# Second attention's preparation: each product of the keys' folded weights directly followed by one of the values

## The chip, the cores and the metric

One core of a Trainium2 chip runs the whole program. The metric is the time of one execution on the device in microseconds (us); the kernel before took 4541.19 us in the median of three runs (4521.63, 4541.19 and 4542.01 us).

## The reference

Four layers follow each other on 8192 tokens of 256 numbers (4 sequences of 2048): an attention with random features, a feed-forward network whose operands are rounded to blockwise FP4, a softmax attention with rotated and low-rank keys and values, and a routed network of 8 experts. The change touches the third layer's inputs only:

```python
q = (x @ wq.T).reshape(b, s, NH, HD).transpose(0, 2, 1, 3)
k = (x @ wk_a.T @ wk_b.T).reshape(b, s, NH, HD).transpose(0, 2, 1, 3)
v = (x @ wv_a.T @ wv_b.T).reshape(b, s, NH, HD).transpose(0, 2, 1, 3)
q = _apply_decoupled_rope(q, cosf, sinf, DROPE)
k = _apply_decoupled_rope(k, cosf, sinf, DROPE)
scores = jnp.einsum('bhqd,bhkd->bhqk', q, k) / np.float32(np.sqrt(HD))
attn = jax.nn.softmax(scores, axis=-1)
```

## The kernel before, in words

`make_plan` (it calls `prep_order` and the other order generators) writes one list of steps. Every engine then goes through that list and issues the steps that have a part for it, strictly in the list's order; semaphores alone tie the engines together. So a step's place in the list is its place on each of the queues.

**Preparation of the second attention.** For each sequence b (0 to 3), in four chunks c of 512 tokens: `pt` transposes the input (two steps), `pa` makes the 64 + 64 latent rows of keys and values (`lat`, rows 0 to 63 for the keys, 64 to 127 for the values), `px` a part of the router's logits, `pp` the queries ("q") and keys ("k") of 128 of the 256 columns (ht is 0 or 1), `ps` splits the float32 result `pres` into three bfloat16 parts on POOL (L1900 to L1906) and stores them with six DMAs from SP, and `pv` makes the values of 128 tokens (j is 0 to 3) and stores them (`vst`, `vdr`). `pp` for the keys multiplies `wkR[0:64]` with `lat[0:64]`, so it stands in the array's rows 0 to 63 and streams 512 columns; `pv` multiplies `lat[64:128]` with `wvb[64:128]`, rows 64 to 127, 256 columns. Each float32 product is recorded as two LDWEIGHTS and two MATMULs. All of these are recorded at one helper's line, L764 (L767 for transposes); they are told apart by their tiles: `lat,wkR` is `pp` of the keys and `wkR,lat` is `pv` (`wvb` and `wkR` share a buffer).

**Where these steps run.** `prep_order` yields small lists; each call of `beside()` or `background()` puts the next one, here called a *slot*, into the plan. A chunk takes 14 slots. Sequence 0 is prepared beside the feed-forward network: from tile T = 20 on there are two slots for each of the 64 tiles T, slot A after the transposes `tt` and ahead of `up`, slot B after `dn`. Sequence 1 starts in the stage that finds the first row maxima (`M` on PE, `MR` on DVE at L1607), 20 slots ahead of the attention's main loop, and goes on in it; sequences 2 and 3 run in the main loop wholly. The main loop has 1024 steps in 16 groups n of 64; a step is `S S M M S S V B` on PE: four score products `S`, each with an exponential on ACT (L1356), two `M`, one `V` (eight MATMULs, four of them side by side) and the slot B, in every other step.

**Banks and waits.** Every `S`, `R1`, `pt`, `pa`, `px`, `pp` and `pv` is an *A step*: PE writes one PSUM bank and ACT empties it. In the main loop they rotate over three banks, and PE waits until ACT has emptied that of three A steps before. Beside the network there is one bank (6), and PE waits until ACT has emptied that of the A step just before:

```python
w.wait_ge(act_A, max(0, a_no[step] - (1 if beside_ffn(step) else 3)))
```

ACT's copy of a `pp` into `pres` also waits until POOL has finished the `ps` before:

```python
w.wait_ge(pool_ps, 4 * (at["ps", b, c, qk] - 1))
```

POOL's `ps` itself waits until the six DMAs of the `ps` before have landed, and `vst` has three buffers, each free when its store has landed. The rows of maxima that an `S` needs come through `R1` (PE, ACT), `R2` (POOL, then eight DMAs `QS<-mrow` from SP, L2082); a group's operands come through `fetch` (SP, L2093 and L2094). `oe` multiplies on POOL (L1844) and waits for the DMA `den<-rd`.

Of the kernel before, what the change touches and what calls it, by code (L numbers as in the profile page):

```python
# [127 lines left out]
def prep_order(b):  # L128

    for c in range(4):  # L130
        for k in range(2):
            yield [("pt", b, c, k)]
        yield ([("pl", *divmod(4 * b + c + 1, 4))] if b and 4 * b + c + 1 < 16 else []) + [("pa", b, c)]
        yield [("px", b, c)]
        for i, w in enumerate("qk"):
            for ht in range(2):
                yield [("pp", b, c, w, ht)]
            yield [("ps", b, c, w)]
            for j in range(2):
                yield [("pv", b, c, 2 * i + j)]  # L140
    yield [("prepared", b)]


# [90 lines left out]
def make_plan():  # L234
# [63 lines left out]
    def beside():  # L298
        units = next(side, None)
        if units:  # L300
            plan.extend(units)
            prepared.update(u[1] for u in units if u[0] == "prepared")
            if 0 in prepared:
                plan.extend(("fm", 0, i) for i in range(4))

    side = prep_order(0)

    for T in range(-1, NT + 7):
# [57 lines left out]


    bg.append(prep_order(1))
    while (0, 0) not in rows:
        maximum()  # L370
# [8 lines left out]
    for step in range(1025):  # L379
        n, st = divmod(step, 64)  # L380
        if st == 0 and n < 16:
            b, g = groups[n]
            if g == 0 and 0 < b < 3:
                bg.insert(0, prep_order(b + 1))
# [1883 lines left out]
```

## Time and profile before

| | |
|---|---|
| Times of three runs, us | 4521.63, 4541.19, 4542.01 |
| Profiled execution, span, us | 4519.8 |
| PE busy | 4297.7 us, 95% |
| DVE busy | 3480.9 us, 77% |
| ACT busy | 2811.6 us, 62% |
| POOL busy | 976.4 us, 22% |
| Chain that ended last | PE 68%, DVE 12%, DMA 3%, issue 2% |

Busy time of PE is the union of its records, in which a product's latency is counted; what a product costs the engine is the distance from its start to the next one's. In the timeline a row gives start, length, engine, line, operation, tiles and how many instructions were merged; in brackets the idle time of the engine ahead of it and what ended it. The idle time of PE's weight loads (PEld) costs nothing while PE multiplies.

### The profile page before, as it was taken

What the parts mean: (1) busy time and instruction counts of PE and PEld (TensorE: products, weight loads), DVE (VectorE), ACT (ScalarE), POOL (GpSimd) and SP (SyncE); (2) the same over time, 40 slices, a digit from 0 to 9 for tenths busy, and PEclk for the clock granted to TensorE, in tenths of its full rate; (3) what the DMA queues carried; (4) which work ended last, traced back from release to release, by engine and by line L of the source; (5) the groups of instructions that cost most, each with busy time, mean ns of one, the idle gap of its engine ahead of it and who ended that gap; (6) DMA issues with size and microseconds to landing.
All of it is one profiled execution on the core that took longest, in us unless ns stands there. A gap on an engine that the chain in (4) does not pass through costs nothing.

```text
span 4519.8 us, 66262 instructions
## 1 busy us (share of the span) xinstructions
PE 4297.7 (95%) x25817; PEld 1630.7 (36%) x25820; DVE 3480.9 (77%) x3858; ACT 2811.6 (62%) x5305; POOL 976.4 (22%) x957
## 2 busy tenths in 40 slices
PE   8899889999989999999999999999999999999896
PEld 5555446666622222222222222222222232222285
DVE  3555789888887788987778888777888988888332
ACT  4333333343347788887777777777777767788721
POOL 3333434454121100001221111111110001000223
PEclk9999999999989999999999999999999999999998
DMA  3102000122133212113232221423222122221232
GB/s 112 35 29 66 20 11 15 65 68 93 57 100 116 69 70 71 42 68 101 99 113 75 82 75 48 136 92 110 67 72 84 45 75 64 71 75 65 95 120 54
DMA packets 230277, 330.49 MB, mean 73 GB/s; under 512 B 36870, under 2 KB 171464, under 8 KB 227912
## 3 DMA queue, kind: packets, MB, share of 16 engines
q1 hardware_dynamic: 227084, 318.40, 21.3%
q0 software_dynamic: 2880, 7.87, 0.9%
q8 instruction: 203, 3.33, 0.3%
q14 instruction: 110, 0.90, 0.1%
HBM read 218.71 MB, written 98.04 MB: 70 GB/s over the span
## 4 chain that ended last, share of the span: by engine, by line
PE 68%; DVE 12%; DMA 3%; issue 2%; POOL 1%; ACT 1%; SPq 1%; POOLq 0%; DVEq 0%; another core or an unknown queue 0%; ACTq 0%
PE ps L764 67%; DVE mx L1607 4%; PE ps L767 2%; DMA pk<-Ob 1%; DVE hn L1428 1%; DVE stat L1434 1%; DVE hn L1586 1%; DVE hn L1581 1%; DMA x2d<-eb 1%; DVE hs L1420 0%; DMA rd<-pk 0%; DMA QS<-mrow 0%; SPq L2082 0%; ACT Pb L1356 0%; DVE eb L1445 0%
## 5 line engine op out<-in xcount | busy, mean ns | idle before, releaser
L1607 DVE TENSOR_REDUCE mx<-ps 128x1 f32<-128x1024 f32 x2048 | 2406.6, 1218 | 423.4 <-PE ps L764 420.2
L1356 ACT ACTIVATE Pb<-ps 128x512 f32<-128x512 f32 x4096 | 2202.5, 596 | 515.1 <-PE ps L764 511.6
L764 PE MATMUL ps<-QS,KS 98*128 98x512 bf16 x4096 | 1248.8, 386 | 17.5 <-ACT Pb L1356 7.7
L764 PE MATMUL ps<-Pb,VA 128*32 128x512 f32 x8192 | 1095.1, 607 | 0.1
L764 PE MATMUL ps<-KM,QM 64*128 64x512 bf16 x4096 | 654.9, 388 | 44.6 <-DVE mx L1607 42.7
L764 PEld LDWEIGHTS ps<-QS,KS 98*128 98x128 bf16 x4096 | 259.6, 98 | 1089.1 <-ACT Pb L1356 907.5
L764 PEld LDWEIGHTS ps<-KM,QM 64*128 64x128 bf16 x4096 | 179.7, 93 | 598.0 <-issue 351.9
L764 PEld LDWEIGHTS ps<-Pb,VA 128*32 128x32 f32 x8192 | 161.3, 108 | 401.4 <-issue 400.4
L1911 POOL CAST mrow<-mres 16x128 bf16<-16x128 f32 x64 | 18.4, 287 | 1238.7 <-ACT mres L1192 1238.7
L764 PE MATMUL ps<-wdT,hT 128*128 128x256 f32 (+1 forms) x768 | 193.8, 395 | 19.3 <-DVE X L1592 19.3
L1514 DVE RECIPROCAL rB<-ps 128x512 f32<-128x512 f32 x28 | 94.0, 3357 | 107.0 <-PE ps L764 106.7
L1844 POOL TENSOR_TENSOR den<-Ob,den 128x512 f32<-128x512 f32 x64 | 81.6, 1275 | 412.9 <-DMA den<-rd 412.9
L764 PEld LDWEIGHTS ps<-wdT,hT 128*128 128x128 f32 (+1 forms) x768 | 140.5, 192 | 72.7 <-issue 50.5
L764 PE MATMUL ps<-wgT,xqT 128*128 128x352 f32 x512 | 164.4, 464 | 0.0
L764 PE MATMUL ps<-wuT,xqT 128*128 128x352 f32 x512 | 161.9, 459 | 0.0
L1900 POOL CAST parts<-pres 128x1024 bf16<-128x1024 f32 x32 | 37.7, 1177 | 479.6 <-ACT pres L1192 474.0
L1837 POOL TENSOR_SCALAR vpe<-mv 128x4 f32<-128x4 f32 (+1 forms) x52 | 12.6, 242 | 592.4 <-DVE mv L1438 592.2
L1213 ACT ACTIVATE phi<-ps 128x1024 f32<-128x1024 f32 x64 | 65.5, 1024 | 114.1 <-PE ps L764 114.1
L764 PEld LDWEIGHTS ps<-wuT,xqT 128*128 128x128 f32 x512 | 97.3, 190 | 54.2
L1565 DVE TENSOR_TENSOR hh<-ps,sg 128x704 f32<-128x704 f32 x64 | 56.5, 882 | 77.5 <-PE ps L764 77.5
L1192 ACT ACTIVATE pres<-ps 128x512 f32<-128x512 f32 x64 | 38.1, 597 | 124.5 <-PE ps L764 121.2
L1502 DVE TENSOR_TENSOR qs<-qs 32x512 f32<-32x512 f32 x128 | 97.0, 758 | 21.6 <-ACT qs L1255 19.3
(235 smaller groups left out, 4312.3 us busy)
## 6 DMA issues: line engine op xcount, KB each, us to landing
QM<-qd SPq DMA_DIRECT2D x128, 256.0 KB
KM<-kd SPq DMA_DIRECT2D x128, 256.0 KB
qd<-parts SPq DMA_DIRECT2D x96, 256.0 KB, 2.7
kd<-parts SPq DMA_DIRECT2D x96, 256.0 KB, 2.7
QS<-qd SPq DMA_DIRECT2D x64, 384.0 KB
KS<-kd SPq DMA_DIRECT2D x64, 384.0 KB
vdr<-vst SPq DMA_DIRECT2D x64, 256.0 KB, 3.1
den<-rd SPq DMA_DIRECT2D x64, 256.0 KB
```

Of the source, the lines that this page charges most:

```text
L764: return eng.matmul(out, a, b, start=start, stop=stop, skip_group_check=skip)
L767: return eng.transpose(out, a, ident[0:n, 0:n])
L1213: eng.activation(phi[n % 3], bank(1, 2), ACT.Exp, bias=0.0, scale=1.0).then_inc(act_phi, 1)
L1356: eng.activation(Pb[(u - 1) % 9], o, ACT.Exp, bias=0.0, scale=0.25).then_inc(act_A, 1)
L1428: eng.tensor_tensor(blk(xn), blk(x), wide(rs, n // 16, 16), ALU.mult).then_inc(own, 1)
L1434: d = eng.bn_stats(stat[:, i % 4, j, :], x[:, j, :])
L1502: d = eng.tensor_tensor(qs[C % 2][g][64 * k + 32 - 32 * g:64 * k + 64 - 32 * g, ht, :], x, x, ALU.mult)
L1514: eng.reciprocal(f["rB"], bank(b7)).then_inc(dve_rec, 1)
L1565: eng.tensor_tensor(hh[p % 2][:, 704 * b:704 * b + 704].rearrange("p (a b) -> p a b", a=2), bank(2, 2).rearrange("p (a b) -> p a b", a=2)[ ...
L1581: eng.scalar_tensor_tensor(out=hn[i], in0=hc, scalar=LEAST, in1=hn[i], op0=ALU.max, op1=ALU.add).then_inc(dve_qh, 1)
L1607: eng.tensor_reduce(mx4[qc % 2][:, 4 * i + q, h:h + 1], o, AX, ALU.max).then_inc(dve_D, 1)
L1844: eng.tensor_tensor(den, Ob, den, ALU.mult).then_inc(pool_at, 1)
```

## The change

Only the order of `prep_order` changes. Each of the keys' two `pp` steps comes together in one slot with one of the first two `pv` steps, `pp` first. `pv` 0 and 1 stood between the queries' `ps` and the keys' first `pp`; now they stand behind the `pp` steps, which come two slots sooner after the queries' `ps`. The keys' `ps` and `pv` 2 and 3 follow as before. A chunk takes 12 slots in place of 14. No instruction is added or removed.

```diff
             yield [("px", b, c)]
-        for i, w in enumerate("qk"):
-            for ht in range(2):
-                yield [("pp", b, c, w, ht)]
-            yield [("ps", b, c, w)]
-            for j in range(2):
-                yield [("pv", b, c, 2 * i + j)]
+        for ht in range(2):
+            yield [("pp", b, c, "q", ht)]
+        yield [("ps", b, c, "q")]
+        for ht in range(2):
+            yield [("pp", b, c, "k", ht), ("pv", b, c, ht)]
+        yield [("ps", b, c, "k")]
+        for j in range(2, 4):
+            yield [("pv", b, c, j)]
     yield [("prepared", b)]
```

## Rows read from the trace of the kernel before

**Rows 1.** The chain that ended last, shares of the span by engine.

```profile
PE 68%; DVE 12%; DMA 3%; issue 2%; POOL 1%; ACT 1%; SPq 1%; POOLq 0%; DVEq 0%; another core or an unknown queue 0%; ACTq 0%
```

**Rows 2.** Busy time by stretch: us, then each engine's, PEclk, DMA share, GB/s.

```profile
core 0: us, PE busy (x) PEld busy (x) DVE busy (x) ACT busy (x) POOL busy (x), PEclk, DMA share, GB/s
800.00:1100.00 300.00, 293.42 (x1203) 194.68 (x1202) 249.54 (x263) 115.00 (x265) 154.03 (x91) 0.98 0.22 74
1265.00:1320.00 55.00, 44.87 (x179) 14.31 (x183) 46.09 (x41) 17.85 (x35) 19.88 (x15) 0.75 0.35 118
2060.00:2372.00 312.00, 311.95 (x1780) 80.57 (x1778) 239.17 (x214) 235.79 (x460) 64.07 (x56) 1.00 0.34 110
```

**Rows 3.** Timeline of the main loop, around a `pv` in slot B.

```profile
2161.15 0.70 PE L764 MATMUL ps<-wkR,lat 64*128 64x256 f32 x2
2161.78 0.61 PE L764 MATMUL ps<-QS,KS 98*128 98x512 bf16 x2
...
2166.14 1.28 POOL L1844 TENSOR_TENSOR den<-Ob,den 128x512 f32<-128x512 f32 x1 [7.42 <-DMA den<-rd]
...
2167.01 0.70 PE L764 MATMUL ps<-wkR,lat 64*128 64x256 f32 x2
```

**Rows 4.** Timeline of the main loop, around a `pp` of the keys.

```profile
2170.68 2.18 ACT L1356 ACTIVATE Pb<-ps 128x512 f32<-128x512 f32 x4 [0.45 <-PE ps L764]
...
2172.88 1.12 PE L764 MATMUL ps<-lat,wkR 64*128 64x512 f32 x2
...
2173.93 0.61 PE L764 MATMUL ps<-QS,KS 98*128 98x512 bf16 x2
2174.10 0.60 ACT L1192 ACTIVATE pres<-ps 128x512 f32<-128x512 f32 x1 [1.24 <-PE ps L764]
...
2174.47 0.61 PE L764 MATMUL ps<-KM,QM 64*128 64x512 bf16 x4
2174.59 2.06 ACT L1356 ACTIVATE Pb<-ps 128x512 f32<-128x512 f32 x4
...
2175.01 0.62 PE L764 MATMUL ps<-QS,KS 98*128 98x512 bf16 x2
```

**Rows 5.** Timeline beside the network, a `pv` in slot B and one in A.

```profile
899.96 0.38 PE L764 MATMUL ps<-wkR,lat 64*128 64x256 f32 x1
900.27 0.33 PE L767 MATMUL ps<-identity,fq 128*128 128x128 f32 x1
...
901.29 0.70 PE L764 MATMUL ps<-wkR,lat 64*128 64x256 f32 x2
...
901.92 2.63 PE L764 MATMUL ps<-wgT,xqT 128*128 128x352 f32 x8
```

**Rows 6.** Timeline beside the network, the keys' two `pp` in slots B and A.

```profile
909.54 1.02 PE L764 MATMUL ps<-lat,wkR 64*128 64x512 f32 x2
...
910.49 0.33 PE L767 MATMUL ps<-identity,fq 128*128 128x128 f32 x1
...
910.66 0.60 ACT L1192 ACTIVATE pres<-ps 128x512 f32<-128x512 f32 x1 [1.73 <-PE ps L764]
...
911.51 1.12 PE L764 MATMUL ps<-lat,wkR 64*128 64x512 f32 x2
```

**Rows 7.** Timeline beside the network: ACT's scaling of X, and a `ps` on POOL.

```profile
892.47 2.06 ACT L1306 ACTIVATE X<-X,shift,rstd 128x256 f32<-128x256 f32 x4
...
892.71 1.04 POOL L1900 CAST parts<-pres 128x1024 bf16<-128x1024 f32 x1 [8.54 <-ACT pres L1192]
...
897.14 2.13 POOL L1906 TENSOR_TENSOR parts<-pres,parts 128x1024 bf16<-128x1024 f32 x1
```

**Rows 8.** Timeline of the stage of the first maxima, sequence 1, chunk 0.

```profile
1262.59 17.25 DVE L1607 TENSOR_REDUCE mx<-ps 128x1 f32<-128x1024 f32 x15 [1.01 <-PE ps L764]
...
1266.55 0.59 PE L764 MATMUL ps<-wkR,lat 64*128 64x256 f32 x2
...
1269.87 2.12 POOL L1906 TENSOR_TENSOR parts<-pres,parts 128x1024 bf16<-128x1024 f32 x1
...
1272.02 1.09 ACT L1192 ACTIVATE pres<-ps 128x512 f32<-128x512 f32 x2 [3.27 <-POOL parts L1906]
```

**Rows 9.** Timeline, SP's and PE's rows at the end of the first group.

```profile
1491.98 3.07 SPq L2059 DMA_DIRECT2D qd<-parts  x6
1495.10 5.32 SPq L2082 DMA_DIRECT2D QS<-mrow  x8
...
1504.97 0.74 SPq L2094 DMA_DIRECT2D KS<-kd  x1
...
1512.76 1.03 PE L764 MATMUL ps<-QS,KS 98*128 98x512 bf16 x2 [4.39 <-DMA KS<-kd]
```

**Rows 10.** Who waited for whom on PE, 1265 to 1700 us: total, times, longest.

```profile
PE ps L764 <- DMA QS<-mrow: 2.0, 1, 2.0
```

## The prediction

> **What bounds the kernel now.** I read the shares of the chain, then busy time by stretch, then who waited on PE, then the timeline around the steps that move. In the chain PE stands for 68% [rows 1]. By stretch [rows 2], PE shows 311.95 of 312 us busy where sequence 2 is prepared in the main loop, and DVE and ACT have about a quarter of the time free; beside the network PE has 293.42 of 300 us and DVE 249.54. So in both places PE's queue sets the pace, and any time that PE spends or stands still comes out at the end. The third place is different: in the stage of the first maxima DVE is nearly always busy (46.09 of 55 us, with PE at a granted clock of 0.75), and its row shows 15 reductions in 17.25 us without a gap [rows 8]. There, work on PE is covered, unless PE stops feeding DVE. The change removes nothing, so I cost each of the three places by itself: 8 pairs beside the network, 3 pairs in front of the main loop (slots 7, 8 and 19, counted from 0, of the 20 there), and 21 in the main loop.
>
> **Main loop, 21 pairs: about nothing.** A `pv` alone holds PE for 0.63 us, from its start to that of the next S (2161.15 to 2161.78) [rows 3]; a `pp` for 1.05 us (2172.88 to 2173.93) [rows 4]. Two slots cost 1.68. If the two halves of rows work at once, the pair costs 1.05: `M` shows it, whose four MATMULs in alternating halves take 0.54 us (2174.47 to 2175.01), as long as the two of S, which use both halves (2173.93 to 2174.47) [rows 4]. But the bank of the second S behind the pair is that of the `pp`, three A steps before. ACT's copy of the `pp` began 1.22 us after the product's start and took 0.60 (2174.10) [rows 4]; with some 0.05 us for the signal, that S can start 1.87 us after the pair's start. With no slot there it would start 0.27 after that moment, half of the 0.54 of two S. So the pair costs 1.87 − 0.27 = 1.60 in place of 1.68. The third S needs the `pv`'s copy, 0.38 later, and stands behind two M (0.54), so it waits for nothing more. The waits at the pair's head are over: ACT ended the four exponentials at 2172.86, when the `pp` began at 2172.88 [rows 4]. Gain 0.08 x 21 = 1.7 us; I take 1, since part of the 0.54 is the turn from M to S and the first S is then longer than the half. It hardly depends on whether the halves overlap: without overlap the pair ends at 1.05 + 0.43 and the same copy is awaited. Bounds: a gain of 0.63 each, 13 us, if ACT's copy were no limit; a loss of 0.3 each, 6 us, if the `pv` holds the `pp`'s end back.
>
> The Trainium skill ("TensorEngine Tiling (Array Packing)", Overview, Theoretical Speedup) promises up to 2x where a dimension is at most 64. By it the pair would cost 1.05. The same page (PSUM Bottleneck) says "Tiling speeds up TensorE but not PSUM evacuation", and the rows on the copy speak for this second sentence.
>
> **Beside the network, 8 pairs: 11 us more.** Here one bank serves all, so the `pv` of a pair can't start until ACT has copied the `pp`. By the plan a chunk starts in slot A both before (every 7 tiles) and after (every 6), so each step keeps its kind of slot but the pairs: `pp` 0 and `pv` 0 come into B, `pp` 1 and `pv` 1 into A. In B a `pv` is free before: the last product of `dn` has 64 rows in the other half, and the `pv`'s second MATMUL starts 0.31 us ahead of the next transposes, as in tiles without it [rows 5]. In A it costs 0.63 (901.29 to 901.92) [rows 5]. In the pair, ACT starts the copy at 910.66, 1.12 after the `pp` began, and ends it at 911.26; the next product would have started at 910.49 [rows 6]. PE stands still for some 0.83 us, then the `pv` takes 0.63. So pair 0 adds 0.83 + 0.63 = 1.46. Pair 1 adds the standstill alone, 0.83, as its `pv` cost 0.63 before too. Four chunks: 4 x 2.3 = 9.2. In two of the four (tiles 30 and 42, remainder 2 by 4) ACT has its scaling of X, 2.06 us [rows 7], and then the copies of `tt` in its queue ahead of the copy of `pp` 1, where PE now waits; that adds some 1.7 twice, 3.4. I take off 1.5 for stretches where the chain goes over DVE. Queued behind the waiting `pv` are `tt` or `up`, for which ACT and DVE wait in turn. One more wait: `pp` 0's copy needs the queries' `ps` to be done. POOL ran it from 892.71 to 899.27, 7.3 us after the `pp` before it; the pair comes one tile later, at 899.6 in this row's tile, and its copy at 900.7 [rows 7]. That holds by 1.4 us, and POOL's contended runs would break it by some 2 us. Bounds: 5 and 20 us.
>
> **In front of the main loop, 3 pairs: 3 us more.** In chunk 0 POOL ends the queries' `ps` at 1271.99, and ACT's two copies of the keys waited 3.27 us for it [rows 8]. PE went on, as no bank was missing. Now `pp` 0 comes in the slot of 1266.55 [rows 8], `pv` 1 a slot and 1.1 us later, and it needs the bank of `pp` 0, which ACT gives at 1272.6. PE stops from about 1268.9 to 1272.7, and DVE, with one `M` in hand, loses some 3.5 us in a stage that it bounds. Chunk 1's first pair comes right ahead of the main loop's first S, with POOL in the middle of the `ps`; I take half of that, 1.5, for it. A `pp` and a `pv` (1.7 us) leave the main loop for this stage. Together 3, bounds −1 and +9.
>
> **The end of sequence 1's preparation: 8 us less.** Eight slots fewer end it at step 55 of group 0 and not at step 7 of group 1. Before, SP was held by the last queries' `ps` until 1491.98, sent the rows of maxima and a group's last keys at 1504.97; PE waited 4.39 us for them and ran two S in 1.03 us in place of 0.61 afterwards, at the lower clock [rows 9]. A wait of 2.0 us for rows is behind another `ps` [rows 10]. Nothing of `prep` is left there now, and both waits should go: 4.4 + 2.0 + some 2.6 for the clock = 9. Against that, some queries' `ps` (chunk 3 here, chunks 0 and 2 later) now stand on POOL one slot behind an `oe`, which ran 5 us after the slot B of its step and ended at 6.3 (2166.14 against 2161.15) [rows 3]. With 6.5 us for the `ps` [rows 7] that is 12.8; the pair's slot comes two slots after that one, at 5.86 each (2161.15 to 2167.01), 11.7, and wants its copy 1.2 later, 12.9. It just fits; I take 1 us off. Net 8 less; bounds 9 less and 3 more. The `finish` steps behind sequences 2 and 3 move by 16 steps; they keep their places within a row of 16, so I cost them at nothing, with 2 us either way.
>
> **Sum.** −1 + 11 + 3 − 8 = +5 us. The profiled execution has a span of 4519.8 us and fits the lowest run, 4521.63. The median of the runs is 4541.19, about 20 us above it, for a reason that this profile can't show. I forecast against the median: 4546. If the changed kernel's median falls on the lower level, it is 4527.
>
> **The rivals.** *The overlap pays in full.* The array's halves work at once and the copies hide: 21 x 0.63 = 13 us less in the main loop, the end of sequence 1 brings its 9, beside the network only its lower bound of 5 more, nothing at the start: −17, or 4524. For it: M's rows. Against: the second S's bank. Chance 0.15. *The one bank costs more* (slower by over 0.5%). Beside the network PE waits for ACT, ACT for POOL's `ps`, and everything queued behind `pp`'s copy, the network's own copies among it, stands: 4 chunks x 4 us more on top of 11, with the start's upper bound of 9 and waits behind `oe` that eat the gain of sequence 1: 11 + 16 + 9 − 1 = +35, 4576. It decides once POOL ends a `ps` more than 1.4 us later after the `pp` than in the rows, and 22.7 us are reached when three of four chunks do. Chance 0.2. *The pairs don't pair.* If the `pv` starts only once the `pp` is over, the main loop costs the same, as worked out; then the time is my forecast, and only the pair's own rows tell. It is inside the forecast's 0.65.
>
> **How the numbers follow.** Forecast 0.65 at 4546, 4532 to 4562 by the terms; the rivals give 4524 and 4576; with the lower level of the runs, 20 us under the forecast, the range is 4515 to 4576. 0.5% is 22.7 us, about what a measurement can tell from no change. Faster by more needs all of the first rival and a lower level as well: 0.08. Slower by more is the second rival and a little of the forecast's upper end: 0.22. The rest is 0.7.
>
> **What would show it.** In the main loop: the distance from a pair's start to the second S behind it is about 1.87 us, with that S released by ACT's copy `pres`; a `pv` record that starts 0.4 us after the `pp` shows the overlap. Beside the network: PE's weight loads of `wkR,lat` wait for `pres`, 0.8 us in B and up to 2.5 in A, and the stretch from 800 to 1100 grows by about 11 us. At the start: PE waits some 4 us for `pres` near 1270, and DVE's run of reductions has a gap. At the end of group 0 no wait for `KS<-kd`. I am wrong if the second S follows the pair without a wait, or if ACT waits for POOL in every chunk.

## The result, and the profile after

The changed kernel took 4590.29 us (median of four runs, 4583.55 to 4604.72) beside 4533.28 for the kernel before: a ratio of 1.0131, 95% interval 1.0113 to 1.0149. It is 57 us slower by the medians. The forecast of 4546 and its range up to 4576 were wrong, and most of the time went where the sum had −1 and 0.

Between the two profiled executions the difference is larger, 83 us: this one has a span of 4602.9 us and is the slowest of its kernel, the one of before (4519.8) is near its lowest. So stages are compared below to see where time goes, and whole kernels by their ratios.

The page's chain of the changed kernel, shares by engine, reads nearly as before [rows 1]:

```profile
PE 68%; DVE 11%; DMA 4%; issue 2%; POOL 2%; ACT 1%; SPq 1%; POOLq 0%; DVEq 0%; another core or an unknown queue 0%; ACTq 0%
```

A share of the whole span doesn't find 57 us. The time by stretch does. Groups 4 and 5 of the changed kernel, each from its first exponential to that of the next:

```profile
core 0: us, PE busy (x) PEld busy (x) DVE busy (x) ACT busy (x) POOL busy (x), PEclk, DMA share, GB/s
2052.00:2266.00 214.00, 204.34 (x1165) 54.97 (x1164) 152.25 (x137) 152.06 (x296) 40.62 (x36) 0.98 0.32 103
2266.00:2476.00 210.00, 195.20 (x1102) 47.17 (x1100) 156.23 (x157) 146.89 (x281) 34.80 (x38) 0.95 0.29 93
```

And the same two groups before:

```profile
2024.00:2224.00 200.00, 199.98 (x1156) 53.97 (x1154) 151.68 (x137) 150.31 (x293) 34.23 (x32) 1.00 0.32 101
2224.00:2417.00 193.00, 192.98 (x1108) 49.04 (x1104) 152.69 (x141) 146.98 (x284) 34.34 (x32) 1.00 0.31 102
```

By the exact borders group 4 takes 14.3 us more and group 5 15.8. PE, which was never idle there [rows 2], now stands for 9.66 and 14.80 us. In group 4 most of the rest is work that came sooner: two of the queries' products, 1.82 us each, which stood in group 5 before (the count of MATMULs goes from 1156 to 1165, and in group 5 from 1108 to 1102). In group 5 it is a lower granted clock (21.7 us at the lower of the two levels). Over groups 4 to 7 the products are the same. Who PE waited for from 1250 to 4220 us, in the changed kernel (total, times, longest):

```profile
PE ps L766 <- DVE mx L1609: 61.5, 75, 4.8
PE ps L766 <- DMA KS<-kd: 31.1, 4, 9.7
PE ps L766 <- ACT pres L1194: 19.4, 21, 5.0
```

Before, `KS<-kd` stood there once, with 4.39 us [rows 9]. `KS<-kd` is the load of a group's keys by `fetch`, and the changed kernel waits for it at the start of groups 5, 6, 9 and 10.

The table divides the difference between the profiled executions by stages. It is read from the starts of one operation that every kernel has at each border: ACT's `sg` of network tiles 20, 56 and 63, and the first exponential `Pb` of groups. The last column is what the prediction had for the stage.

```
                                        after   predicted
beside the network, tiles 20 to 56      +17.4   +11  (bounds 5, 20)
tile 63 to the start of group 0          +8.2    +3  (bounds -1, 9)
group 0 to the middle of group 1         -0.7    -8  (bounds -9, 3)
groups 4 to 7   (sequence 2 prepared)   +28.5   -0.5 \ main loop, and
groups 8 to 11  (sequence 3 prepared)   +25.9   -0.5 / finish at 0 +- 2
ahead of tile 20, and the rest           +3.9     0
```

The first three stages together have 25 us where the sum had 6; the next two have 54 where it had −1. Of these, groups 4, 5, 8 and 9 carry 14 to 16 each; groups 6 and 10 have 1.7 more, groups 7 and 11 3.3 and 3.8 less. In groups 4 to 11 all of PE's waits come to 61.0 us, before to 16.5. So 44.5 of the 54 us are waiting: 31.1 for `KS<-kd`, 10.4 more for DVE's maxima (24.1 in place of 13.7), 5.8 for `pres`, and 2.8 less for the rows of maxima. The rest comes with the lower clock, less what the pairs save: 61.4 us at the lower level, before none.

**The bank.** This part of the working came out as told. The changed kernel's PE in the main loop (start, duration, operation; in brackets the idle time before and its releaser), with ACT's copy:

```profile
2178.60 0.69 PE L766 MATMUL ps<-lat,wkR 64*128 64x512 f32 x1
2178.61 0.70 PE L766 MATMUL ps<-wkR,lat 64*128 64x256 f32 x2
2179.14 0.59 PE L766 MATMUL ps<-lat,wkR 64*128 64x512 f32 x1
2179.66 0.39 PE L766 MATMUL ps<-QS,KS 98*128 98x512 bf16 x1
...
2179.82 0.60 ACT L1194 ACTIVATE pres<-ps 128x512 f32<-128x512 f32 x1 [1.24 <-PE ps L766]
...
2180.47 0.39 PE L766 MATMUL ps<-QS,KS 98*128 98x512 bf16 x1 [0.43 <-ACT pres L1194]
```

The two products begin 0.01 us apart, and the first S follows 1.06 after their start, as long as a `pp` alone takes [rows 4]: the row halves work at once. (The recorded sign of it was a `pv` that starts 0.4 us after the `pp`; it starts 0.01 after.) The second S waits for `pres` and comes 1.87 us after the pair's start, the predicted figure.

**SP's queue.** This is what the prediction missed. The changed kernel at the start of group 5, POOL's last operation of a `ps`, SP's issues and PE:

```profile
2251.36 2.13 POOL L1908 TENSOR_TENSOR parts<-pres,parts 128x1024 bf16<-128x1024 f32 x1
...
2253.52 3.08 SPq L2061 DMA_DIRECT2D qd<-parts  x6
2256.63 0.80 SPq L2095 DMA_DIRECT2D QS<-qd  x1
2257.47 0.76 SPq L2096 DMA_DIRECT2D KS<-kd  x1
...
2265.70 1.03 PE L766 MATMUL ps<-QS,KS 98*128 98x512 bf16 x2 [8.07 <-DMA KS<-kd]
```

And before, the same issues:

```profile
2209.57 0.79 SPq L2093 DMA_DIRECT2D QS<-qd  x1
2210.40 0.76 SPq L2094 DMA_DIRECT2D KS<-kd  x1
```

Group 5 began at 2223.5 then, so the keys' load was issued 13 us ahead of its group. Now the queries' `ps` of chunk 2 stands at step 61 of the group's 64, and `fetch` at the same step behind it. SP's rows come in the plan's order: the six stores of the `ps` must wait for POOL until 2253.52, the load goes out at 2257.47, and PE, which would have started group 5 at 2257.63, stands for 8.07 us. Its first two S then take 1.03 us in place of 0.61, at the lower clock. Group 9 begins in the same way, after 9.70 us.

Groups 6 and 10 begin late for a second cause of the same kind. The changed kernel at the start of group 6:

```profile
2457.37 3.66 POOL L1880 TENSOR_SCALAR eb<-eb,shift 128x256 f32<-128x256 f32 x4
...
2461.06 0.39 SPq L2151 DMA_DIRECT2D out_y<-eb  x1
...
2464.86 0.76 SPq L2096 DMA_DIRECT2D KS<-kd  x1
...
2475.09 1.03 PE L766 MATMUL ps<-QS,KS 98*128 98x512 bf16 x2 [7.16 <-DMA KS<-kd]
```

Here it is a `finish` step (`of`), whose store of the output waits for POOL. It stands ahead of `fetch` since `finish` comes 16 steps earlier.

### The profile page after: what moved, and what is told of

Read it like the earlier page. It is cut to its first block, busy times and chain, and to the rows that moved or that the text cites. A ratio compares the mean times of both kernels' runs of the same rounds, so it can differ in the third digit from the quotient of the medians.

```text
span 4602.9 us, 66260 instructions
## 1 busy us (share of the span) xinstructions
PE 4322.0 (94%) x25817; PEld 1637.5 (36%) x25820; DVE 3473.5 (75%) x3858; ACT 2814.9 (61%) x5305; POOL 969.9 (21%) x957
## 4 chain that ended last, share of the span: by engine, by line
PE 68%; DVE 11%; DMA 4%; issue 2%; POOL 2%; ACT 1%; SPq 1%; POOLq 0%; DVEq 0%; another core or an unknown queue 0%; ACTq 0%
PE ps L766 66%; DVE mx L1609 4%; PE ps L769 2%; DMA pk<-Ob 2%; DMA KS<-kd 1%; DVE stat L1436 1%; DVE hn L1430 1%; DMA den<-rd 1%; DVE hn L1588 0%; ACT pres L1194 0%; DVE hn L1583 0%; DMA ypar<-eo,tabs 0%; DVE eb L1447 0%; ACT Pb L1358 0%; POOL pres L1904 0%
## 5 line engine op out<-in xcount | busy, mean ns | idle before, releaser
L766 PE MATMUL ps<-QS,KS 98*128 98x512 bf16 x4096 | 1259.0, 388 | 53.4 <-DMA KS<-kd 31.1
L766 PE MATMUL ps<-wdT,hT 128*128 128x256 f32 (+1 forms) x768 | 191.8, 392 | 13.6 <-DVE X L1594 13.6
L766 PEld LDWEIGHTS ps<-wgT,xqT 128*128 128x128 f32 x512 | 98.1, 201 | 52.7 <-issue 15.0
```

Of the source, the lines that this page charges most:

```text
L766: return eng.matmul(out, a, b, start=start, stop=stop, skip_group_check=skip)
```

## The experiments

Four theories stood against each other once the traces lay side by side: that the pairs themselves cost the time (the bank wait, and the lower clock behind it); that the places in SP's queue do, which the shorter preparation moves; that the clock alone does; and that the part beside the network, not the main loop, carries the loss. Each ratio is to the kernel before, measured beside it. A stage is read from one profile, and the clock moves it: with sequence 0 in the old order the stage of tiles 20 to 56 came out at 0.0, −3.3 and −4.3 us in other executions.

### Which sequences carry it

**New order for sequence 0 alone** (the 8 pairs beside the network), the old one for the others:

```diff
+        if b == 0:
             for ht in range(2):
                 yield [("pp", b, c, "q", ht)]
...
+        else:
+            for i, w in enumerate("qk"):
...
```

> The new order for sequence 0 alone (beside the network), the old one for the others. Profiles of before and after differ by 17.4 us from tile 20 to tile 56 of the network, of which PE's waits for the copy of pres are 12 us and the rest goes with 27 us more at the lower clock. If the cost is made there by itself: +17 to +21 us against before, and nothing behind. If part of the loss behind the network came from a later start of sequence 1: more than that. My sum on record has +11 for it.

Measured: 4545.3 us, a ratio of 1.0031 (1.0013 to 1.0049), 14 us and so a little under the expected 17 to 21, inside the interval. Its profile has the same 17.4 us from tile 20 to tile 56.

**New order for sequences 1 to 3 alone**, the same edit with `if b:`.

> The old order for sequence 0, the new one for 1 to 3. By the stages of the two profiles: +8 in front of the main loop, -1 in group 0, +28 in groups 4 to 7, +26 in groups 8 to 11, so +55 to +62 us. If the delay beside the network caused some of it, less. My sum on record has -6 for it.

Measured: 4584.55 us, 1.0120 (1.0099 to 1.0142). That is 54 us, at the lower edge of what was expected; groups 4 to 11 have 53.7 of it in the profile. The two parts add up to 1.015 beside 1.013 for the whole, within their intervals. So four fifths of the loss lie in the sequences 1 to 3, where the prediction had a gain.

### The pairs, or the places

**Pairs with the old places.** Two empty slots behind the queries' `ps` keep the chunk at 14 slots, so that all that comes behind stays at its step:

```diff
         yield [("ps", b, c, "q")]
+        yield from [[]] * 2
         for ht in range(2):
             yield [("pp", b, c, "k", ht), ("pv", b, c, ht)]
```

> Pairs in all sequences, with two empty slots behind the queries' ps, so that a chunk keeps 14 slots and every ps its old place on SP and POOL. If the losses of the main loop are made by SP's order (a group's last fetch behind a ps or an of) and not by the pairs: groups 4 to 11 lie within 3 us of before, no wait for KS<-kd above 5 us, and the 3 us waits for POOL beside the network are gone; what is left is the bank's wait beside the network, +9 to +15 us. If the pairs themselves cost (bank, turning of the array): groups 4 to 11 stay some 20 us and more above before.

Measured: 4541.69 us, 1.0025 (1.0009 to 1.0041), as expected for the case that the places make the loss of the main loop. Beside the network the pairs that waited 3.2 us for POOL wait 1.0 and 0.75 here, and another one 2.0.

**The new places without pairs.** Twelve slots again, the products of values beside the `ps` steps, which have none of their own on PE:

```diff
-        yield [("ps", b, c, "q")]
+        yield [("ps", b, c, "q"), ("pv", b, c, 0)]
+        yield [("pv", b, c, 1)]
         for ht in range(2):
-            yield [("pp", b, c, "k", ht), ("pv", b, c, ht)]
-        yield [("ps", b, c, "k")]
-        for j in range(2, 4):
-            yield [("pv", b, c, j)]
+            yield [("pp", b, c, "k", ht)]
+        yield [("ps", b, c, "k"), ("pv", b, c, 2)]
+        yield [("pv", b, c, 3)]
```

> 12 slots a chunk without any pair: pv 0 and 2 share a slot with the two ps, which have no part on PE. The queries' ps and all that follows sequence 2 and 3 stand where the change has them. If the shift of places makes the loss: waits for KS<-kd of 6 to 10 us at the starts of groups 5, 6, 9 and 10 as with the change, +35 to +55 us from group 4 to 12, and nothing beside the network. If the pairs make it: no such waits and the time of before.

Measured: 4555.79 us, 1.0056 (1.0035 to 1.0078). By stage (us against before, between profiled executions):

```
                                      after   pairs, old   new places,
                                              places       no pairs
tiles 20 to 56                        +17.4    +13.8        -4.3
tile 63 to group 0                     +8.2     -0.1        +6.8
group 0 to the middle of group 1       -0.7     +3.8        -9.1
groups 4 to 7                         +28.5     +0.1       +21.0
groups 8 to 11                        +25.9     -1.1       +20.4
```

The pairs cost time beside the network, where one bank serves all. The places cost it in sequences 2 and 3, and at the start too. But the two don't add up to the change: 0.25% and 0.56% are 0.81%, and the change has 1.31%. Some 0.5%, 23 us, comes only where both are present. In groups 4 to 11 the new places alone have 41.5 us, the old places with pairs −1.0, the change 54.4. Beside the places alone, the change there waits 10.3 us more for DVE's maxima (24.1 beside 13.8) and 5.8 for `pres`, and stands 61 us at the lower level in place of 44. What makes PE wait more for DVE wasn't taken apart. PE's waits from 1250 to 4220 us with pairs at the old places:

```profile
PE ps L767 <- ACT pres L1195: 8.3, 21, 0.4
PE ps L767 <- DMA QS<-mrow: 5.1, 3, 3.0
PE ps L767 <- DMA KS<-kd: 4.9, 1, 4.9
```

and at the new places without pairs:

```profile
PE ps L766 <- DMA KS<-kd: 30.8, 5, 8.9
```

The 21 waits for `pres` are the 21 pairs at up to 0.43 us each. They cost nothing net: groups 4 to 11 are 1.0 us shorter than before in sum. The 31 us for `KS<-kd` come with the places, pairs or not. The clock is no cause by itself either: in groups 4 to 11 PE is never at the lower level before or with the pairs at old places, for 44 us with the new places and 61 with the change, so that it goes with the waits.

### Where the load stands in SP's queue

**The change with `fetch` four steps earlier:**

```diff
-FETCH = 14
+FETCH = 10
```

> The change, with FETCH 10 in place of 14: a group's fetches stand four steps sooner in the plan, so the last one (step 58) is on SP's queue ahead of the queries' ps of step 61 and of the of of step 59. If SP's order makes the losses: the waits for KS<-kd at the starts of groups 5, 6, 9 and 10 (8.1, 7.2, 9.7, 6.2 us) and the time at the lower clock behind them vanish, 30 to 42 us less than the change has, so +15 to +28 against before; what is left is the cost beside the network, the start's, and PE's wait for DVE of 4.6 us in groups 5 and 9. If the loads are late for another reason (traffic), the waits stay.

Measured: 4559.7 us, 1.0069 (1.0051 to 1.0087).

**The kernel before with the same edit**, as a control.

> Control: the kernel before with FETCH 10. It has one wait for KS<-kd (4.4 us at the start of group 1) and about 2.6 us at the lower clock behind it. Gone: -5 to -7 us; nothing else moves. If sooner fetches help in themselves, more than that.

Measured: 4546.05 us, 1.0032 (1.0019 to 1.0044). So the edit costs the kernel before 14 us, where 5 to 7 less had been expected, and saves the changed one about 28, a little under the expected 30 to 42. The waits show both. First the changed kernel with it, then that of before with it:

```profile
PE ps L766 <- DMA QS<-mrow: 20.7, 9, 6.8
PE ps L766 <- ACT pres L1194: 17.1, 23, 4.0
```

```profile
PE ps L764 <- DMA QS<-mrow: 22.2, 11, 4.1
```

No wait for `KS<-kd` is left, and a new one has come. `QS<-mrow` are the rows of maxima, which SP issues in 5 us; they stood ahead of the load before, now stand behind it, and PE waits for them. One queue serves all, so what is put forward there holds back something else. A remainder of 0.37%, 17 us, stays over the control. In groups 4 to 11 the changed kernel with the edit is 20 us longer than before, its control 13; the change alone was 54. So with `fetch` out of the way, sequences 2 and 3 pay some 8 us for the new order in place of 54. Beside the network it is +10.2 and at the start +10.7, and from group 0 to the middle of group 1 −9.7, the gain that the change didn't have.

**The change one slot later in sequences 2 and 3.** If it is the places, one step should do much:

```diff
+    if b > 1:
+        yield []
     for c in range(4):
```

> The change, with one empty slot ahead of sequences 2 and 3, so that all their steps come two steps later and the queries' ps of chunk 2 stands at step 63, behind the group's last fetch (61) on SP. If that one place makes the losses of groups 4 and 8 (14.3 and 14.4 us in the change's profile): both fall to under 3 us, and the waits for KS<-kd at the starts of groups 5 and 9 go; those at the starts of groups 6 and 10 (behind the of, now at 61, still ahead of the fetch) stay at 6 us or grow. In all 26 to 32 us less than the change, +25 to +33 against before. If the density of the DMAs in a chunk of 12 slots makes the loss, the waits stay, wherever the ps stands.

Measured: 4569.03 us, 1.0073 (1.0052 to 1.0094), 0.6% off the change for one empty slot in each of two sequences. PE's waits:

```profile
PE ps L768 <- ACT pres L1196: 19.5, 23, 4.0
PE ps L768 <- DMA KS<-kd: 6.2, 3, 2.9
```

Groups 4 and 8 are now 3.7 us longer each than before in place of 14.3 and 14.4, groups 5 and 9 9.0 and 6.9 in place of 15.8 and 13.6. The waits for the keys fell from 31.1 to 6.2 us. The `pres` waits did not change, and the time did. That rules them out as the main cause. A chunk's DMAs come as densely as in the change, so their density isn't it either. Of the 3.7 us that groups 4 and 8 still have, the two queries' products that came sooner are 3.6.

One part came out otherwise than expected: the waits at groups 6 and 10, behind `of`, were to stay at 6 us or grow, since `of` still stands ahead of the load, and fell to 2.9 and 2.8. At group 6:

```profile
2433.13 0.76 SPq L2098 DMA_DIRECT2D KS<-kd  x1
...
2441.39 0.60 PE L768 MATMUL ps<-QS,KS 98*128 98x512 bf16 x2 [2.93 <-DMA KS<-kd]
```

PE was ready for the group at 2438.46. The load went out 5.3 us ahead of that (3.1 with the change) and PE started 8.3 us after its issue (10.2). So the order of `of` and load alone doesn't set the size of the wait.

### What the pair is worth with the other product first

In the change the second S waits for the bank of the keys' `pp`. If the values' product goes first, the second S takes the bank of that one, which is done and copied sooner.

**Value first, in 14 slots, all sequences:**

```diff
+        yield from [[]] * 2
         for ht in range(2):
-            yield [("pp", b, c, "k", ht), ("pv", b, c, ht)]
+            yield [("pv", b, c, ht), ("pp", b, c, "k", ht)]
```

> As e3 (pairs in all sequences, 14 slots), but the pv ahead of the pp. In the main loop the second S then needs the bank of the pv, whose product and copy are shorter (about 0.4 + 0.4 us), the pp's bank is needed only by the third. If the bank's wait is what eats the overlap: PE's 21 waits for pres (8.3 us in e3) go, and a pair saves 0.5 to 0.6 us, 10 to 13 us less than e3 from group 0 to 12. If the array's halves don't give the time: the same as e3. Beside the network the pp waits for the copy of the pv, 0.38 us and not 0.60, and in slot B the pv hides beside dn: 3 to 6 us less than e3's +13.8 there.

Measured: 4525.81 us, 0.9991 (0.9978 to 1.0003), beside 1.0025 with the keys first. In the profiles that is 7.7 us from group 0 to group 12, where 10 to 13 had been expected, and 7.7 beside the network, where 3 to 6 had.

**The same, with sequence 0 in the old order:**

> The pairs with pv first and 14 slots for sequences 1 to 3, the old order for sequence 0. Should hold the gain alone: 10 to 13 us less than before (ratio 0.997 to 0.998) if the bank's theory is right, 0 to 2 less if it is not. Nothing beside the network.

Measured: 4517.09 us, 0.9973 (0.9964 to 0.9983). PE at a pair of this kernel:

```profile
2173.64 0.48 PE L775 MATMUL ps<-wkR,lat 64*128 64x256 f32 x1
2173.64 0.69 PE L775 MATMUL ps<-lat,wkR 64*128 64x512 f32 x1
2173.96 0.38 PE L775 MATMUL ps<-wkR,lat 64*128 64x256 f32 x1
2174.18 0.59 PE L775 MATMUL ps<-lat,wkR 64*128 64x512 f32 x1
2174.70 0.61 PE L775 MATMUL ps<-QS,KS 98*128 98x512 bf16 x2
2175.24 0.61 PE L775 MATMUL ps<-KM,QM 64*128 64x512 bf16 x4
```

Both S follow with no wait, and M comes 0.54 behind them. ACT ended the values' copy at 2174.81, when the second S was not yet due. The pair takes 1.06 us where two slots took 1.68 [rows 3, 4]: 0.62 x 21 pairs in the main loop = 13 us, and the ratio of 0.9973 says 12. In the profile, groups 4 to 11, with 16 of the pairs (9.9 us by this figure), are 7.1 us shorter, with 6.8 us at the lower level where before had none. So the overlap is real, and in the changed kernel the bank wait ate it. Beside the network no order helps: value first waits there too (6.6 us in 8), and leaving that sequence alone is worth 0.18%.

**Sequence 1 in 12 slots, value first.** Without pairs the new places gave 9.1 us at the end of sequence 1's preparation, as forecast; in the changed kernel they gave almost nothing. So this kernel adds to the last one, for sequence 1 only:

```diff
+        if b == 1:
...
+            yield [("ps", b, c, "q")]
+            yield []
+            for ht in range(2):
+                yield [("pv", b, c, ht), ("pp", b, c, "k", ht)]
+            yield [("ps", b, c, "k")]
+            yield [("pv", b, c, 2), ("pv", b, c, 3)]
```

> e8 (pv first, 14 slots), but sequence 1 in 12 slots a chunk, its pv 2 and 3 in one slot and one empty slot behind the queries' ps: its ps of chunk 3 stand at steps 45 and 53, not at 57 and 3. If a ps at 57 ahead of the fetch at 61 makes the wait of 4.4 us at the start of group 1 with the lower clock behind it: 5 to 8 us less than e8, ratio 0.995 to 0.997. A rival: the ps at 21 and 29 meet the fm loads (27 to 39), which delay rows or pk by some us; then no gain over e8.

Measured: 4514.01 us, 0.9949 (0.9934 to 0.9963), faster than both kernels and some 11 us under the last one by the ratios, where 5 to 8 had been expected. From group 0 to the middle of group 1 it is 12.7 us shorter than before, and it gives 4.6 back ahead of group 0.

## Why the prediction was wrong, step by step

- **What bounds the kernel: right.** PE's queue sets the pace in both places, and where PE stopped, the kernel got longer.
- **Main loop, 21 pairs: right in mechanism and size** for what it priced. The 1.87 us are there to the hundredth; the waits came to 0.43 each; groups 4 to 11 with pairs at the old places are 1.0 us shorter (forecast 1 for all 21 pairs). For the case without overlap the working adds 0.43 us for the `pv`, where rows 3 have 0.63; with that too the pair ends ahead of the 1.87 us, and nothing changes. The Trainium skill ("TensorEngine Tiling (Array Packing)", PSUM Bottleneck: "Tiling speeds up TensorE but not PSUM evacuation") agrees with the kernel with keys first. But it is not the whole story: with the product that is copied fastest put first, its other rule (Overview, Theoretical Speedup, up to 2x) holds, and the pair costs 1.06 in place of 1.68, 1.6 times as fast, a case that the working did not look at.
- **The failed step: "they keep their places within a row of 16, so I cost them at nothing, with 2 us either way".** The sentence is about `finish`. The same was done, without a sentence, for the preparation steps of sequences 2 and 3, which move too: of them the working asked what PE, ACT and POOL do (it names their queries' `ps` one slot behind an `oe`), and not what then stands ahead of `fetch` on SP. A place within 16 steps says which other steps share the slot. It doesn't say what comes near the group's end, where `fetch` is due at step 61. The queries' `ps` of chunk 2 went to that step, and `of` to step 59. The prediction had read this mechanism itself, in rows 9: SP held by a `ps`, the keys' load behind it, PE waiting 4.39 us. It used it once, as a gain for sequence 1, and did not ask whether the same now happens to sequences 2 and 3. The loads behind the `ps` made PE wait 8.07 and 9.70 us, those behind `of` 7.16 and 6.19, and with the lower clock and the other waits the two sequences have 54 us. By the ratios, all that the places do, with their share at the start and at sequence 1, is 0.56%, 25 us, without pairs, and 1.0131 − 1.0025, 48 us, with them. It was entered as 0.
- **Beside the network: 17.4 in place of 11**, inside its bounds. Six of the eight waits were the predicted ones. The changed kernel, from 828 us:

```profile
828.79 1.02 PE L766 MATMUL ps<-lat,wkR 64*128 64x512 f32 x2
...
830.56 0.70 PE L766 MATMUL ps<-wkR,lat 64*128 64x256 f32 x2 [0.75 <-ACT pres L1194]
...
898.31 1.02 PE L766 MATMUL ps<-lat,wkR 64*128 64x512 f32 x2
...
899.71 2.12 POOL L1908 TENSOR_TENSOR parts<-pres,parts 128x1024 bf16<-128x1024 f32 x1
...
901.86 0.60 ACT L1194 ACTIVATE pres<-ps 128x512 f32<-128x512 f32 x1 [7.75 <-POOL parts L1908]
...
902.51 0.70 PE L766 MATMUL ps<-wkR,lat 64*128 64x256 f32 x2 [3.19 <-ACT pres L1194]
```

  The short waits, 0.69 to 0.75, were forecast as 0.83. The extra for ACT's scaling of X (1.7 twice, at the second pair of a chunk) did not come: all second pairs wait 0.69. In its place the `ps` on POOL was late in two chunks of the four, and PE waited 3.19 and 3.18 us at their first pair: the condition of the rival "the one bank costs more" came true in half the chunks. That the waits sum to about what was priced is in part luck. All eight come to 10.6 us, and from tile 20 to tile 56 PE waits 5.7 us less for DVE's X than before (2.2 beside 7.9). What the sum lacked is the clock: there PE was at its lower level for 37.5 us, before for 10.2.
- **In front of the main loop: 8.2 in place of 3**, inside its bounds of 9. The changed kernel:

```profile
1288.76 1.02 PE L766 MATMUL ps<-lat,wkR 64*128 64x512 f32 x2
...
1293.10 0.60 ACT L1194 ACTIVATE pres<-ps 128x512 f32<-128x512 f32 x1 [6.71 <-POOL parts L1908]
...
1293.75 0.79 PE L766 MATMUL ps<-wkR,lat 64*128 64x256 f32 x1 [3.97 <-ACT pres L1194]
...
1333.66 0.60 ACT L1194 ACTIVATE pres<-ps 128x512 f32<-128x512 f32 x1 [6.71 <-POOL parts L1908]
...
1334.32 0.61 PE L766 MATMUL ps<-QS,KS 98*128 98x512 bf16 x1 [3.15 <-ACT pres L1194]
```

  The first wait, 3.97, is the forecast's "some 4 us". The one for chunk 1 was entered at half of that and is 3.15. These two waits need both halves of the change: pairs at the old places have neither and lost nothing here (−0.1), and new places without pairs have neither. Those lost 6.8 all the same, in another way: one wait of 2.6 us for ACT, which waited for a store of the values, and 48.4 us at the lower level in place of 30.7.
- **End of sequence 1: nothing in place of 8.** The wait for `KS<-kd` at group 1 did go, and between step 48 of group 0 and the middle of group 1 the changed kernel is 14.4 us shorter. But it was 13.6 longer by step 48. Some of that is only work that comes sooner, as in the new places without pairs, which are 7.1 longer there with no wait at all and 9.6 us at the lower level in place of 3.4. Another part is this, in the changed kernel:

```profile
1489.35 1.27 POOL L1846 TENSOR_TENSOR den<-Ob,den 128x512 f32<-128x512 f32 x1 [22.45 <-DMA den<-rd]
...
1491.35 0.69 PE L766 MATMUL ps<-lat,wkR 64*128 64x512 f32 x1
...
1494.98 2.12 POOL L1908 TENSOR_TENSOR parts<-pres,parts 128x1024 bf16<-128x1024 f32 x1
...
1497.79 0.61 PE L766 MATMUL ps<-QS,KS 98*128 98x512 bf16 x1 [5.00 <-ACT pres L1194]
```

  An `oe` that waits for its load holds POOL, the `ps` behind it, ACT's copy behind that, and the pair's bank. The working had this chain and said "It just fits; I take 1 us off", by 0.1 us. It did not fit. New places without the pairs had the full 9.1. But with `FETCH` 10 the same pairs in the same order had 9.7: there this `oe` starts 147.3 us after the group's start in place of 153.5, not held by its load, and no wait for `pres` is above 1.4 us. So it is the `oe` held by its load that broke the fit, and the pairs alone don't bring it. The change and its relatives with the same order in this stage go from −0.7 over −3.2 (sequences 1 to 3 alone) and −5.6 (a slot later) to −9.7, with longest waits for `pres` of 5.0, 5.6, 4.0 and 1.4 us and 18.0, 14.5, 11.9 and 8.3 us at the lower level.
- **The range** left out what no term held. With a term of some 50 us entered as 0 ± 2, its upper end was 14 us short.

What stays open: why pairs and new places together cost 23 us more than the two by themselves, and with it why PE waits more for DVE's maxima in groups 5 and 9 (6.5 and 6.7 us; 1.7 each with the new places alone). How much of the lower clock behind a wait belongs to that wait is not settled either: in groups 4 to 7 PE was at the lower level for 34.1 us, in 8 to 11 for 27.3. And one profile of each kernel leaves a term of the stage from group 0 to the middle of group 1 known to some 5 us only.

## What to carry to other kernels

When steps are taken out of a schedule, list for each queue (SP and POOL above all) what now stands just ahead of a step with a due time; here the new places, with stores that wait for a slow engine in front of loads that the next stage needs, cost two to four times what the overlap can save (25 us without the pairs, 48 with them, against 12). Don't add up two halves of a change from runs of each alone: here 0.25% and 0.56% made 1.31%. Two products in the two row halves of TensorE do run at once, and what they save is kept only if the instruction behind them doesn't want the bank whose copy was started last: putting the shorter product first turned +0.25% into −0.09% with nothing else changed. Cost a shared queue by both ends: bringing `fetch` forward took 31 us of PE's waits for it away and brought 21 for the loads behind it, and it made the kernel before 14 us slower.

## What the runs showed of the hardware

- **Short stops of PE and its clock.** Waits of 0.69 to 3.2 us beside the network, eight of them, 10.6 us in all, stand beside 27 us more at the lower of TensorE's two levels (1.2 GHz in place of 2.4). How often it happens varies: sequence 0 is the same in four kernels, which had 37.5, 37.5, 20.5 and 20.5 us at the lower level, and lost 17.4, 17.4, 10.2 and 10.4 us in the stage. All of PE's waits there were 12.7 to 12.9 us in each of the four, so the loss goes with the time at the lower level, and a stop costs more than its length.
- **Loads land late when it matters.** The keys' load (384 KB) was issued at 2257.47 and PE started behind it at 2265.70, 8.2 us later; at group 6 10.2 us. Of the 13 us that it had before, 8 to 10 were needed.
- **A pair in pieces.** The records show each float32 product of a pair as two MATMULs, in turn, and the S behind it 1.06 us after both starts. The longer product alone takes 1.05 [rows 4], so the second one came free, to 0.01 us.
